# A convolution's Toeplitz strips loaded in two transfers, and its products ordered long and short in turn

## The reference, cut to what matters

```
x = x + conv(x)          # per head: causal convolution with a kernel K[h, 0:512] made from
                         # exp() of 64 complex modes, plus D[h] * x, masked by a length per sample
x = x + lora(x)          # x @ W.T + bias + (x @ A[id].T) @ B[id].T, id per sample
```

## Time and profile before

| what | value |
|---|---|
| median of 3 runs | 209.57 us (209.55 to 209.66) |
| profiled execution | 209.66 us |
| its span, first to last instruction | 207.6 us |
| PE busy | 189.7 us, 91% |
| weight loads busy | 165.7 us, 80% |
| DVE busy | 168.7 us, 81% |
| DMA, whole span | 56.47 MB, mean 272 GB/s |

### The profile page before, as it was taken

One profiled execution on the slowest core, in us unless ns is written; L12 is line 12 of the kernel. 1 busy time (PEld: TensorE's weight loads), 2 busy tenths in 40 slices (PEclk: granted clock), 3 DMA queues, 4 the chain that ended last, 5 costly groups with the idle time before them and its releaser, 6 DMA issues.

```text
span 207.6 us, 4381 instructions
## 1 busy us (share of the span) xinstructions
PE 189.7 (91%) x1054; PEld 165.7 (80%) x1054; DVE 168.7 (81%) x370; ACT 121.1 (58%) x354; POOL 90.8 (44%) x144
## 2 busy tenths in 40 slices
PE   0049999999999999899999999999999999999993
PEld 0037899999999999788888888888888888888883
DVE  3985698689699997869998788887888878888662
ACT  2798964334546446266775756656666666756530
POOL 4850000002275788078565545446454464544500
PEclk9999999999999999999999999999999999999999
DMA  5984999999999999965876766667666666764334
GB/s 140 384 331 118 348 406 413 407 412 407 409 412 411 407 407 415 379 219 163 288 253 213 240 200 216 204 215 233 202 229 197 223 218 202 227 203 175 102 101 155
DMA packets 21666, 56.47 MB, mean 272 GB/s; under 512 B 3283, under 2 KB 3987, under 8 KB 21395
## 3 DMA queue, kind: packets, MB, share of 16 engines
q1 hardware_dynamic: 18146, 47.55, 61.9%
q0 software_dynamic: 2560, 8.39, 13.3%
q10 hardware_dynamic: 944, 0.36, 0.8%
HBM read 45.64 MB, written 10.65 MB: 271 GB/s over the span
## 4 chain that ended last, share of the span: by engine, by line
PE 81%; DMA 9%; DVE 5%; POOL 1%; issue 1%; SPq 1%; DVEq 0%; ACTq 0%
PE z_ps L945 24%; PE y_ps L983 20%; PE k_ps L983 20%; DMA strip<-k_pad 8%; PE z_ps L971 7%; PE y_ps L1010 2%; PE y_ps L1009 2%; PE k_ps L1010 2%; PE k_ps L1009 2%; DMA par<-params 1%; DMA k_pad<-k_sb 1%; SPq L263 1%; PE y_ps L1032 1%; PE k_ps L1032 1%; PE y_ps L993 1%
## 5 line engine op out<-in xcount | busy, mean ns | idle before, releaser
L945 PE MATMUL z_ps<-xp,strip 128*128 128x512 f32 (+3 forms) x384 | 63.7, 327 | 0.7 <-DMA strip<-k_pad 0.6
L945 PEld LDWEIGHTS z_ps<-xp,strip 128*128 128x128 f32 x384 | 59.3, 197 | 4.9 <-DMA strip<-k_pad 1.1
L417 POOL DMA_INDIRECT b_hl<-b_tab,b_idx x32 | 38.0, 1186 | 16.5 <-issue 8.8
L412 POOL CAST ag<-a_hl 128x128 fp32r x64 | 23.5, 370 | 38.9 <-PE z_ps L971 28.2
L983 PE MATMUL k_ps<-w_hi,xp 128*128 128x512 f32 x120 | 39.5, 390 | 0.0
L983 PE MATMUL y_ps<-w_hi,xp 128*128 128x512 f32 x120 | 39.5, 390 | 0.0
L552 ACT ACTIVATE ag<-a_hl 128x64 fp32r x128 | 25.7, 249 | 21.1 <-issue 20.9
L750 DVE TENSOR_TENSOR xp<-z_all,xp 128x512 fp32r<-128x512 f32 x32 | 27.6, 862 | 5.2 <-ACT xp L462 5.2
L462 ACT ACTIVATE xp<-z_all 128x512 fp32r<-128x512 f32 x32 | 19.8, 627 | 17.1 <-PE z_ps L945 15.6
L983 PEld LDWEIGHTS y_ps<-w_hi,xp 128*128 128x128 f32 x120 | 22.6, 188 | 4.2
L983 PEld LDWEIGHTS k_ps<-w_hi,xp 128*128 128x128 f32 x120 | 22.6, 188 | 4.2
(11 more groups left out here) (139 smaller groups left out, 236.9 us busy)
## 6 DMA issues: line engine op xcount, KB each, us to landing
strip<-k_pad SPq DMA_DIRECT2D x30, 512.0 KB, 8.4
z_all<-x_conv SPq DMA_DIRECT2D x16, 512.0 KB, 8.8
x_t<-x_tile SPq DMA_DIRECT2D x32, 256.0 KB, 2.8
out<-a_raw SPq DMA_DIRECT2D x31, 256.0 KB, 2.5
strip<-k_pad SPq DMA_DIRECT2D x4, 256.0 KB, 3.6
a_raw<-a_t SPq DMA_DIRECT2D x2, 512.0 KB, 8.5
x_t<-b_rows SPq DMA_DIRECT2D x2, 512.0 KB, 9.0
w_sb<-w_t SPq DMA_DIRECT2D x2, 512.0 KB, 9.8
```

The costliest lines, as they stand in the source:

```text
L412: last = g.tensor_copy(ag[:, s, :, :, q, :].rearrange("p c e r -> p e c r"), src)
L417: g.indirect_dma_start(out=b_hl[:, t % BS, :].bitcast(F32), out_offset=None, in_=b_tab, in_offset=bass.IndirectOffsetOnAxis(ap=b_idx[:, t: ...
L945: last = nc.tensor.matmul(z_ps[:, h % ZS, m * P:L], strip[:, h % SS, m * P:(m + 1) * P, t], xp[:, h % XS, 0:LC - m, e, :], start=(n == 0), ...
```

## The change

From the seventh strip on (head 6, where a slot is used for the second time) a strip is loaded in two transfers: columns 64 to 511 of all 128 partitions (3584 B each), and columns 0 to 63 of partitions 64 to 127 (512 B each). Columns 0 to 63 of partitions 0 to 63 are always zero, and the slot's first strip has put zeros there. Both transfers count on the slot's semaphore, and PE waits for the sum. The twelve products of a head are ordered in pairs: for heads from 2 on 512 and 128 columns in turn (m = 0 and 3), six of them, and then 384 and 256 in turn (m = 1 and 2). For heads 0 and 1, whose strips come in halves, m = 0 and 1 in turn, and then m = 2 and 3.

```diff
+CORNER = P // 2
...
-            def load_strip(h, s, j0, j1, done):
+            def load_strip(h, s, j0, j1, done, p0=0):
 
-                src = bass.AP(tensor=k_pad.tensor, offset=k_pad.offset + 2 * (h * PAD + 1 + j0),
-                              ap=[[2, P], [1, 2 * (j1 - j0)]])
-                sp.dma_start(strip[:, s, j0:j1, :].rearrange("p l e -> p (l e)").bitcast(F32), src).then_inc(done, 16)
+                src = bass.AP(tensor=k_pad.tensor, offset=k_pad.offset + 2 * (h * PAD + 1 + p0 + j0),
+                              ap=[[2, P - p0], [1, 2 * (j1 - j0)]])
+                sp.dma_start(strip[p0:P, s, j0:j1, :].rearrange("p l e -> p (l e)").bitcast(F32), src
+                             ).then_inc(done, 16)
...
                     load_strip(h, h, L // 2, L, strip_landed[h])
+                elif h < SS:
+                    load_strip(h, h, 0, L, strip_landed[h])
                 else:
-                    load_strip(h, h % SS, 0, L, strip_landed[h % SS])
+                    load_strip(h, h % SS, CORNER, L, strip_landed[h % SS])
+                    load_strip(h, h % SS, 0, CORNER, strip_landed[h % SS], CORNER)
...
+            def paired(longer, shorter):
+
+                kinds = ((0, 0), (0, 1), (1, 0))
+                return [(m, t, e) for m0, m1 in zip(longer, shorter) for t, e in kinds for m in (m0, m1)]
+
...
-                    pe.wait_ge(strip_landed[h % SS], 16 * (h // SS + 1))
+                    pe.wait_ge(strip_landed[h % SS], 16 + 32 * (h // SS))
...
-                terms = [(m, t, e) for m in range(LC) for t, e in ((0, 0), (0, 1), (1, 0))]
+                terms = paired((0,), (1,)) + paired((2,), (3,)) if h < 2 else paired((0, 1), (3, 2))
                 for n, (m, t, e) in enumerate(terms):
 
-                    if h < 2 and (m, t, e) == (LC // 2, 0, 0):
+                    if h < 2 and n == len(terms) // 2:
                         pe.wait_ge(strip_landed[h], 16)
```

## The result

The changed kernel takes 212.04 us (median of 4 runs, 211.36 to 212.97) against 209.61 us of the kernel before (4 runs, 209.55 to 209.66). The ratio is 1.0105, 95% interval 1.0082 to 1.0129: slower by about 1%, where 209.3 us and "within 0.2%" were forecast, and above the range (211.2). The profiled execution is the slowest of the four: 212.97 us, span 210.9.

A forecast was written before the change was run, and what follows sets the result against it. PE (1.96 us a head) and a full DMA queue were taken to run almost level. Order 0, stall of head 26 -0.26, behind the heads 0: about -0.3 us from 209.57, so 209.3 us, range 208.5 to 211.2.

The forecast's parts named there:

- the price of the small transfer: Strips 6 to 31: shorter rows save 156 ns, the added corner costs 115 ns per engine, net -0.04 us a strip.
- The bound of +0.07: Upper price of a split strip, if the rows lie on 8 engines only or two engines share one way.
- the 0.26 us: PE's idle time before head 26, forecast to go since the queue would be 0.84 us earlier there: -0.26 us.
- the corner costs more than it saves: Rival: at +0.07 us a strip the queue is 1.5 us later at strip 26, giving 211.0 us; chance 0.29.
- The order: Products of a head in pairs: a load waits for its predecessor's product to start, so costed at 0, heads 1.96 us.
- the 0.01 allowed: Possible change by the product order, 0.01 us a head either way, 0.3 us over 32 heads.
- full 0.06 us waits: PE's wait for weights behind each 128-column product, 0.06 us, forecast to remain in the new order.
- The stall of head 26: Named as PE's only remaining wait for DMA in the stage; it would vanish, -0.26 us and no more.
- SP's issues: 26 transfers more at 0.43 us each, covered by SP's waits for PE and the queue's lag: nothing.
- Behind the heads: The gain is passed on to the tiles, with the first gather of b the nearest limit: 0.

The follow-up runs named there:

- rows spread: Against the change, the small transfer's 64 rows go to every second partition, by an alternating layout: 210.53 us, ratio 1.0025 to the kernel before.
- two transfers of 64 rows: Against the change, strips in two transfers: even (3584 B) and odd partitions (4096 B), ratio 0.9999; or partitions 0 to 63 and 64 to 127, whole, 1.1748.
- the transfers alone: Against the change, strips still in two transfers but the products in the old order: 212.28 us, ratio 1.0106 to the kernel before.
- the order alone: Against the change, whole strips in one transfer as before, the new order of products kept: 210.01 us, ratio 1.0018 to the kernel before.
- the versions with the reordered source: Runs with the alternating partition layout, the host ordering the rows of x to match; for instance even and odd partitions, 210.06 us, ratio 0.9999.
- the version with W later: Whole strips and the new order, with the two W loads issued after strips 26 and 28 instead of 24 and 27: 209.89 us, ratio 0.9998.
- the small transfer first: The change with its two transfers issued the other way round: 212.09 us, ratio 1.0097 to the kernel before.
- all rows: Against the change, the small transfer loads columns 0 to 63 for all 128 partitions: 211.92 us, ratio 1.0105 to the kernel before.
- column halves: Against the change, whole strips as two transfers of all partitions, columns 256 to 511, then 0 to 255: 212.04 us, ratio 1.0083.

## Why the prediction was wrong

**The forecast step that failed** is the price of the small transfer, -0.04 us a strip, which rests on rows that "spread over all 16 engines" like those of a whole strip. It was worked out from the number and size of packets, and with rows spread over all partitions that is what it measured (-0.044). With the rows in partitions 64 to 127 it measured +0.085 with the old order, and +0.085 (by the 16th additions) to +0.135 (by the last) in the profiled run of the change. The bound of +0.07, for rows on 8 engines only or for engines that share one way into the lower partitions, was the right one to lean to: no row of the trace showed a transfer to half of the partitions, and the choice between the ends was made from a row that spoke of size alone. The runs show that the place of the rows matters (rows spread -0.044 against +0.085; two transfers of 64 rows 0.9999 against 1.1748); they don't show by which path inside. Of the bound's two reasons, the first would not by itself make a packet longer, and packets are longer (rows of 3584 B take 153 ns on average against 144 with rows spread). The page "DMA: Bandwidth & Descriptors" of the Trainium skill, in its section "The descriptor swizzle", describes each engine of a 128-partition transfer as writing one port of the memory, with partitions 0 to 63 on the even and 64 to 127 on the odd ports. From this one would expect a transfer to one half to load half of the ports. A rate of 240 against 410 GB/s agrees with that, and that every second partition is fast agrees too. The advice in the section "Rules for kernel authors" of the same page of the Trainium skill, against two transfers for partition halves, held, and by far more than sharing the engines would give.

**What became of the 0.26 us.** The prediction had the queue 21 x 0.04 = 0.84 us earlier at strip 26, and the wait there gone. In the run of the transfers alone strip 26 ends 2.0 us later than before. 0.4 of it stands at strip 5, before any strip is split; the other 1.6 have come up bit by bit since, as 21 x 0.08 us. In the profiled run of the change it is 3.1 us: the mean of the additions is 1.8 us later, and their spread has grown from 2.1 to 3.9 us, which puts the last one another 1.3 us behind. That spread is 2.7 us at strip 7 already and keeps growing, where it is about 2 us all along with the old order. Nothing is paid once for a second transfer: in the kernels that split strips without using one half of the partitions, the last addition is as late as the packets' price says.

**The rival** "the corner costs more than it saves" had the sign, the place and the mechanism: 1.5 us later at strip 26, 1.6 measured in the transfers alone. Its 211.0 us was too low by 1.0, for a price of 0.085 instead of 0.07 (0.3 us over 21 strips), for first strips that came 0.2 to 0.4 us later in these two traces, and in the profiled run for the wider spread. How much of the spread is in the median of 212.04 is not known.

**The order.** Its reading was right in the mechanism: a load never runs ahead by more than one, and a short product costs 0.12 us wherever it stands. "Nothing" was off by 0.027 us a head: 1.933 in each kernel with the new order, 1.960 with the old. That is beyond the 0.01 allowed, in steps of 0.01 to 0.02 us that the two decimals of the timeline do not carry. It is no effect of the full 0.06 us waits, which are still there, and its cause stays open. One reading was too round: heads 8 and 15 start 2.62 us behind the head before, with products of `k_ps` in between, and not 1.96; this is so in both orders (2.60 in the new one) and changes no term. What came of it was zero, as the queue binds at head 21 and 26 (the order alone: 1.0018). The page "TensorE: Matmul & The Clock Gate" of the Trainium skill (Architectural detail), by which loads are pulled ahead of running matmuls, is not borne out here for more than one load ahead.

**The stall of head 26** as the place that decides: right, and it grew instead of vanishing. It is not alone: in the changed kernel PE also waits for strips at heads 14, 19, 20, 21 and 28. **SP's issues** were costed at nothing. They did grow: SP's wait for PE fell from 25.7 us to 13.4, and an issue at 48.72 took 1.31 us. The chain of the changed kernel puts them on the path from 47 to 53 us. But strip 20, whose first part was issued at 52.30 instead of 51.41, ended 2.2 us later than before (63.07 against 60.86), and strip 19 had already ended 2.1 us later. There is no jump where the issues come late, so the queue's lag covered them, as assumed. The chain shows who released whom, not what would have been sooner. Where SP's issues do cost is at the first strips, in the versions with the reordered source.

**Behind the heads** the gain or loss passed on, and the first gather was rightly named as next: it took the gain of the version with W later.

Open: by which path rows in one half of the partitions slow the queue, and why the spread of a strip's additions grows to 4 us in the profiled run of the change, is 2.7 to 3.3 us with the small transfer first, and stays at 2 us with the old order. There is one trace of each, and no run isolates it.

## What to carry to other kernels

Before a transfer is split, ask of each part which partitions it goes to: rows for one half of the partitions take more time than their bytes and packets say, and on a full queue they slow all that follows; if a part of the rows must be loaded apart, lay the data out so that they are every second partition. When two transfers count on one semaphore, the 16th addition need not be the landing of the first: compare the last addition with the last addition of the one transfer that they replace. And if two resources run level, a gain in one (here 0.027 us a head on PE) is only worth what the other leaves room for.

## What was not expected of the hardware

- Two transfers of 64 neighbouring partitions brought the queue from 410 to 240 GB/s at a DMA share of 1.04; the same number of rows in every second partition, half of them 512 B shorter, ran at 400. The share of busy time does not tell them apart.
- The 16 additions of one whole strip, 4096 B to each of 128 partitions, come over 2.1 us on a full queue (71.63 to 73.71). A second transfer behind the first makes this little longer (strip 26: 2.2 us with all rows, 2.1 with rows spread, 2.7 with column halves).
- The same twelve products take 1.933 or 1.960 us by their order alone.
- A source with a reordered row step takes SP about 0.6 us to issue, 0.43 otherwise.
